# Layer 1's attention scores from float32 operands in groups of 32 rows, in a two-layer transformer kernel on one core

## What is computed

```python
# plain, and cosine with normalised q and k; a rotary turn came before
scores = einsum('bhtd,bhsd->bhts', q, k) * scale + causal
# hyperbolic
tq = sqrt(1 / curv + sum(q * q)); tk = sqrt(1 / curv + sum(k * k))
inner = einsum('bhtd,bhsd->bhts', q, k) - tq * tk.T
dis = sqrt(1 / curv) * arccosh(max(-curv * inner, 1 + 1e-7))
scores = 1 / (1e-6 + dis) + causal
# all
out = softmax(scores) @ v
```

## Time and profile before

| | |
|---|---|
| median of three executions | 2942.42 us |
| the profiled execution | 2944.73 us |
| its span, first to last instruction | 2942.8 us |
| mean granted clock of TensorE, of full speed | 0.814 |
| instructions | 30130 |
| DMA | 128.32 MB, 14.8% of 16 engines' span |

### The profile page before, as it was taken

One profiled execution on the slowest core, in us unless ns is written; L12 is line 12 of the kernel. 1 busy time (PEld: TensorE's weight loads), 2 busy tenths in 40 slices (PEclk: granted clock), 3 DMA queues, 4 the chain that ended last, 5 costly groups with the idle time before them and its releaser, 6 DMA issues. The chain is left out here.

```text
span 2942.8 us, 30130 instructions
## 1 busy us (share of the span) xinstructions
PE 2303.2 (78%) x10649; PEld 866.6 (29%) x10649; DVE 1553.3 (53%) x3429; ACT 1378.9 (47%) x1963; POOL 657.2 (22%) x639
## 2 busy tenths in 40 slices
PE   3799847777999884777798987667789998477789
PEld 1222321223433341122343234121334223212134
DVE  2553446675456354666455526467545634466642
ACT  1145315893134531788224452288622453248932
POOL 1012101332321210233241120033223111013324
PEclk8599866678999885777799987578689998667789
DMA  5100220001400022000330003110032002200012
GB/s 142 40 18 2 73 71 30 17 1 50 128 23 18 16 66 77 27 6 1 95 98 25 2 22 87 50 32 1 12 112 70 18 1 73 67 21 30 1 34 90
DMA packets 67750, 128.32 MB, mean 44 GB/s; under 512 B 11300, under 2 KB 24740, under 8 KB 62980
## 3 DMA queue, kind: packets, MB, share of 16 engines
q1 hardware_dynamic: 67600, 126.40, 14.8%
HBM read 109.99 MB, written 15.20 MB: 43 GB/s over the span
## 5 line engine op out<-in xcount | busy, mean ns | idle before, releaser
L1279 DVE TENSOR_REDUCE mx<-ps 128x1 f32<-128x512 f32 (+3 forms) x1248 | 644.0, 552 | 562.3 <-PE ps L629 468.6
L1008 ACT ACTIVATE pr<-ps 128x1024 f32<-128x1024 f32 (+3 forms) x672 | 515.9, 804 | 537.0 <-PE ps L699 534.4
L626 PE MATMUL ps<-kop,qop 72*128 72x512 bf16 (+6 forms) x1248 | 441.3, 372 | 158.2 <-DVE mx L1279 90.1
L699 PE MATMUL ps<-qop,kop 75*128 75x512 bf16 (+7 forms) x1344 | 409.8, 370 | 160.2 <-DMA kop<-parts_scratch 56.5
L745 PE MATMUL ps<-pr,vt 128*32 128x512 f32 (+3 forms) x2688 | 442.8, 590 | 5.2 <-POOL pr L1563 4.6
L1563 POOL TENSOR_SCALAR_AFFINE_SELECT pr<-pr 128x512 f32<-128x512 f32 x224 | 145.9, 651 | 987.5 <-ACT pr L1008 986.1
L1063 ACT ACTIVATE pr<-ps 128x512 f32<-128x512 f32 x224 | 133.8, 597 | 405.1 <-PE ps L851 316.4
L626 PEld LDWEIGHTS ps<-kop,qop 72*128 72x128 bf16 (+1 forms) x1248 | 124.7, 101 | 608.0 <-DVE mx L1279 342.8
L861 PE MATMUL ps<-pr,w_down 128*128 128x512 f32 x384 | 211.5, 638 | 69.6 <-POOL pr L1554 48.8
L699 PEld LDWEIGHTS ps<-qop,kop 75*128 75x128 bf16 (+1 forms) x1344 | 123.4, 105 | 380.3 <-ACT pr L1008 122.4
L848 PE MATMUL ps<-hT,w_gate 128*128 128x512 f32 x384 | 205.5, 618 | 0.0
(11 more groups left out here) (298 smaller groups left out, 3012.3 us busy)
## 6 DMA issues: line engine op xcount, KB each, us to landing
wb<-gates_scratch SPq DMA_DIRECT2D x192, 256.0 KB, 3.3
qop<-parts_scratch SPq DMA_DIRECT2D x96, 192.0 KB
kop<-parts_scratch SPq DMA_DIRECT2D x96, 192.0 KB
on<-hmax_scratch SPq DMA_DIRECT2D x8, 1024.0 KB, 5.5
parts_scratch<-on SPq DMA_DIRECT2D x24, 256.0 KB, 3.4
parts_scratch<-wb SPq DMA_DIRECT2D x24, 256.0 KB, 2.9
xin<-in_x SPq DMA_DIRECT2D x4, 512.0 KB, 4.5
on<-in_cos SPq DMA_DIRECT2D x4, 512.0 KB, 3.8
```

The lines of the kernel that those rows point to most:

```text
L626: mm = pe.matmul(o, qop[0:k, slot(l, u), j, qb * P:(qb + 1) * P], kop[0:k, slot(l, u), j, k0:k0 + wd], start=True, stop=not diag)
L699: mm = pe.matmul(o, kop[0:k, slot(l, u), 2 * pair + j, kb * P:(kb + 1) * P], qop[0:k, slot(l, u), 2 * pair + j, q0:q0 + wd], start=True, s ...
L1008: nc.scalar.activation(pr[:, g % 3, 2 * pair:2 * pair + 2, o0:o0 + wd], ps[:, bank:bank + 2, o0:o0 + wd], ACT.Exp).then_inc(a.exps, 1)
L1279: ins_ = nc.vector.tensor_reduce(mx[:, nth(l, u) % 2, j, qb, col % 2:col % 2 + 1], ps[:, bank, 0:wd], AX.X, ALU.max, negate=True)
```

## The change

In layer 1, q and k stay float32. `qop` and `kop` are seen as `q32` and `k32`, [128 rows, 4 units, 1024]; head j of a unit has rows 32j to 32j+7. Row 32j+8 (`MROW`) holds the row maximum in `q32` and ones in `k32`; for the hyperbolic unit row 32j+8 holds ones in both, and 32j+9 (`TROW`) holds tq or tk. 32 DMAs copy head by head from where q and k were computed. A score is one float32 product of 8, 9 or 10 rows, placed at row 32j of the array. The maxima of units 1 and 2 are turned in float32 and stored by one DMA. Layer 0 is as before, but its rows of ones are loaded again in each batch, since layer 1 overwrites them. The core of the diff:

```diff
+        q32, k32 = (op[:, 0:2].rearrange("p s j n -> p (s j n)").bitcast(F32).rearrange("p (u n) -> p u n", u=UNITS)
+                    for op in (qop, kop))
-        trow = [on[0:36, 3, 0:CH].bitcast(BF16), on[0:36, 2, 0:CH].bitcast(BF16)]
+        trow = [on[0:4, 1, :], on[0:4, 2, :]]
 setup, SP and POOL
+                sp.wait_ge(s_ones, 1)
+                sp.dma_start(ones_dram, k32[MROW::32]).then_inc(s_stored, 16)
+                sp.wait_ge(s_stored, 16)
+                sp.wait_ge(s_ones, 2)
-                nc.gpsimd.memset(kop[:], 1.0)
+                nc.gpsimd.memset(k32[:], 1.0).then_inc(s_ones, 1)
+                pool.wait_ge(s_stored, 16)
+                nc.gpsimd.memset(kop[:], 1.0).then_inc(s_ones, 1)
 PE, rows of tq and tk
-                            mm = pe.matmul(ps[0:36, (6 if side else 2) + t // 4, (t % 4) * P:(t % 4 + 1) * P],
-                                           tp9[:, t, side], identb[:], start=True, stop=True)
+                            col = 4 * (NT * side + t)
+                            mm = pe.matmul(ps[0:4, (6 if side else 2) + t // 4, (t % 4) * P:(t % 4 + 1) * P],
+                                           tT[:, col:col + 4], w["ident"][:], start=True, stop=True)
 PE, pieces
-                        mm = pe.matmul(o, qop[0:k, slot(l, u), j, qb * P:(qb + 1) * P],
-                                       kop[0:k, slot(l, u), j, k0:k0 + wd], start=True, stop=not diag)
+                        if l:
+                            rows = slice(32 * j, 32 * j + (TROW + 1 if is_hyp(l, u) else HD))
+                            mm = pe.matmul(o, q32[rows, u, qb * P:(qb + 1) * P], k32[rows, u, k0:k0 + wd],
+                                           start=True, stop=not diag, tile_position=(32 * j, 0))
 PE, scores (hyp_scores likewise, with TROW + 1)
+                            if l:
+                                rows = slice(32 * h, 32 * h + (MROW + 1 if has_max(l, u) else HD))
+                                mm = pe.matmul(o, k32[rows, u, kb * P:(kb + 1) * P], q32[rows, u, q0:q0 + wd],
+                                               start=True, stop=True, tile_position=(32 * h, 0))
 DVE, prepare: both splits go, and the split and copies of the rows of tq and tk
-                    dve.wait_ge(factors_used, i + 1)
-                    operand_parts(1, 3 * i, parts[:, i], dsts[i], tmp)
-                link(split(by_tile(tT), lambda k: tp[:, :, :, k, :], by_tile(tU)))
-                for i in range(3):
-                    nc.vector.tensor_copy(q9[:, :, i], tp[:, :, 0])
-                    ins_ = nc.vector.tensor_copy(k9[:, :, i], tp[:, :, 1, i].unsqueeze(2).broadcast_to([P, NT, 3, 4]))
 DVE, maxima of standard units: no split
+                    if l and not is_hyp(l, u):
+                        ins_.then_inc(a.nmp, 1)
+                        return
 SP
+            def move_heads(side, u):
+                src, dst = (on[:, 0, :], kT[:])[side], (q32, k32)[side]
+                for j in range(4):
+                    h = HD * (4 * u + j)
+                    sp.dma_start(dst[32 * j:32 * j + HD, u, :], src[h:h + HD, :]).then_inc(at[1].ops[u], 16)
 SP, send_maxima
+                if l:
+                    sp.dma_start(q32[MROW::32, u, :].rearrange("j (q n) -> j q n", n=P),
+                                 hrow[:]).then_inc(at[1].maxrow[u], 16)
+                    return
 SP, layer 0's start; before layer 0's gates; after them
+                sp.dma_start(kop[MAXROW:MAXROW + 3, 0:2].rearrange("p s j n -> p s (j n)"),
+                             ins["onerow"][0:1].rearrange("a j n -> a (j n)").unsqueeze(1).broadcast_to(
+                                 [3, 2, 4 * N])).then_inc(at[0].one_rows, 16)
-            sp.dma_start(qop[MAXROW:MAXROW + 3, slot(1, HYP_UNIT), :, :], ins["onerow"]).then_inc(
-                at[1].ops[HYP_UNIT], 16)
+            sp.dma_start(k32[MROW::32], ones_dram).then_inc(at[1].one_rows, 16)
+            sp.dma_start(q32[MROW::32, HYP_UNIT, :], ones_dram[:, 0]).then_inc(at[1].one_rows, 16)
             for side in range(2):
-                store_parts(1, side, 3 * side, parts[:, side])
-            for u in (0, HYP_UNIT, 1):
-                load_unit(1, u)
+                sp.wait_ge(factors_used, side + 1)
+                for u in (0, HYP_UNIT, 1, 2):
+                    move_heads(side, u)
+            for dst, row, ready in ((q32, trow[0], t_row), (k32, trow[1], t_krow)):
+                sp.wait_ge(ready, 1)
+                sp.dma_start(dst[TROW::32, HYP_UNIT, :], row).then_inc(at[1].ops[HYP_UNIT], 16)
             for c in range(NC):
                 spread_hyp_maxima(c)
             send_maxima(1, b + 1 < B, 1, BOTH)
-            sp.wait_ge(at[1].pv, NS)
-            load_unit(1, 2)
             send_maxima(1, b + 1 < B, 2, BOTH)
```

More of the change, by code:

```diff
@@ L18 @@
 MAXROW = PAIRS
-TROW = PAIRS + 3
-K_MAX, K_HYP = PAIRS + 3, PAIRS + 3 + 9
+K_MAX = PAIRS + 3
 LN_EPS = 1e-5
@@ L46 @@
 NP_ = len(PIECES)
-OPS = 16 * 6
-OPS_HYP = OPS + 16 * (1 + 2)
+OPS = (16 * 6, 16 * 8)
+OPS_HYP = OPS[1] + 16 * 2
+MROW, TROW = HD, HD + 1
 def diagonals(g):
@@ L481, in __init__ @@
                     self.proj, self.proj_used = sem(n + "proj"), sem(n + "proj_used")
-                self.parts = sem(n + "parts")
-                self.stored = [sem(n + f"stored{i}") for i in range(2)]
+                else:
+                    self.parts = sem(n + "parts")
+                    self.stored = [sem(n + f"stored{i}") for i in range(2)]
+                self.one_rows = sem(n + "one_rows")
                 self.v = sem(n + "v")
@@ L714, in hyp_scores @@
                     for j in range(2):
[L715 to L718, removed]
+                        h = 2 * (k % 2) + j
+                        rows = slice(32 * h, 32 * h + TROW + 1)
+                        mm = pe.matmul(ps[:, bank + j, o0:o0 + wd], k32[rows, HYP_UNIT, kb * P:(kb + 1) * P],
+                                       q32[rows, HYP_UNIT, q0:q0 + wd], start=True, stop=True,
+                                       tile_position=(32 * h, 0))
                     mm.then_inc(h_prod, 1)
@@ L1126, in split, with operand_parts @@
                 return nc.vector.tensor_tensor(dst(2), r, dst(1), ALU.subtract)
-            def operand_parts(l, first, p, src, r):
-                done = at[l].parts
+            def operand_parts(first, p, src, r):
+                done = at[0].parts
                 nc.vector.tensor_copy(p[:, 0, :], src).then_inc(done, 1)
@@ L1232, in maxima @@
                                                        ALU.min)
+                    if l and not is_hyp(l, u):
+                        ins_.then_inc(a.nmp, 1)
+                        return
                     link(ins_)
-                    if is_hyp(l, u):
+                    if l:
                         c = chunks[0]
@@ L1619, in sync_program, with load_rows @@
         def sync_program(sp, b):
-            def load_rows(l, u, side, i):
+            def load_rows(u, side, i):
                 op = (qop, kop)[side]
-                heads = scratch[l, side, :, :, 4 * u:4 * u + 4, :].rearrange("i d h n -> i d (h n)")
+                heads = scratch[side, :, :, 4 * u:4 * u + 4, :].rearrange("i d h n -> i d (h n)")
                 if side:
@@ L1627, in load_rows, with load_unit, store_parts @@
                     src = heads.rearrange("i d n -> (i d) n")
[L1628 to L1633, removed]
+                sp.dma_start(op[24 * i:24 * i + 24, slot(u), :, :].rearrange("p h n -> p (h n)"),
+                             src).then_inc(at[0].ops[u], 16)
+            def load_unit(u):
                 for side in range(2):
                     if u == 0:
-                        sp.wait_ge(a.stored[side], 48)
+                        sp.wait_ge(at[0].stored[side], 48)
                     for i in range(3):
[L1638 to L1641, removed]
-                        sp.dma_start(op[TROW:TROW + 9, slot(l, u), :, :], rows).then_inc(a.ops[u], 16)
-            def store_parts(l, side, first, p):
+                        load_rows(u, side, i)
+            def move_heads(side, u):
[3 more added lines that the diff above has]
+                    sp.dma_start(dst[32 * j:32 * j + HD, u, :], src[h:h + HD, :]).then_inc(at[1].ops[u], 16)
+            def store_parts(side, first, p):
                 for i in range(3):
-                    sp.wait_ge(at[l].parts, first + i + 1)
-                    sp.dma_start(scratch[l, side, i].rearrange("d h n -> h d n"), p[:, i]).then_inc(
-                        at[l].stored[side], 16)
+                    sp.wait_ge(at[0].parts, first + i + 1)
+                    sp.dma_start(scratch[side, i].rearrange("d h n -> h d n"), p[:, i]).then_inc(
+                        at[0].stored[side], 16)
             def gate_rows(l, guest):
```

78 lines of the change are left out of this document (42 added, 36 removed).

## The result

The changed kernel takes 3576.64 us (median of four runs, 3575.58 to 3581.00), against 2942.96 for the kernel before: 1.2159 times as long, 95% interval 1.2135 to 1.2182. The forecast was 2928, its range ended at 3035. Two executions of the kernel before, beside the first run of experiment 8, were in a slow state (3703.63 and 8405.29 us) and are left out of its median.

What follows compares the result with a forecast made beforehand. PE was busiest overall, but the stage had an empty start, a lower-clock PE stretch and ScalarE-bound stretches. -19.3 and +14.5 gave -4.8 a batch, -19 in four; with +4.5 setup, 2928 us, range 2862 to 3035.

Steps and rivals of the forecast that it cites:

- Term 1: Start of layer 1's attention stage: bf16 splits go and first pieces start earlier, about -19.3 us per batch.
- Term 3: Setup, once: POOL fills k32, waits for its store, then fills kop; DVE last before; +4.5 us.
- Term 2: PE's work in layer 1's attention stage: float32 columns cost four times bf16's, partly regained by overlap; +14.5 us a batch.
- The lower clock that slows it now should go once PE has no gaps.: Positions 2 to 5 of the stage: 39.8 us becomes 42, +2, with the lower clock expected to go.
- that cover would just do: Positions 22 to 27, 36.1 us: hidden by ScalarE's 34.46 even if PE stayed at the lower clock; change 0.
- Three of the signs named beforehand: Forecast wrong if stretches grow over 25 us a batch or nothing, or POOL's fill doesn't end after DVE; clock near 1 expected.
- every rival: Whole kernel: forecast case 2900 to 2960 us (0.43); others 2876 (0.19), 3002 (0.20), 3110 (0.12), 2967 (0.06).
- Rival D: Layer 1's attention: row groups don't overlap, pairs run in series, 18.5 plus 27 us a batch, 3110 us; chance 0.12.
- Work in columns: PE's stage work counted at the upper clock: 1.67 ns a float32 column, 0.42 a bf16 one.
- Pairs overlap: Adjacent score pairs in different row groups overlap as column groups do: 0.98 us start to start, not 1.72.
- Pieces hidden, a quarter to a third: Pieces in another row group hide beside score pairs: 2, 5, 4.5, 3 and 7 us by stretch.
- Tile changes, 0.22 us a mask at the upper clock: Two more tile changes of about 0.11 us at each mask product, 80 a stage: 18 us.

Runs made afterwards that it cites:

- experiment 8: Kernel before with q's loads moved ahead of k's stores: alone 2923.56 us (ratio 0.9925); with layer 1's products also widened to 128 rows 2883.44 us (0.9787).
- Experiment 7: Kernel before, layer 1's scores and pieces reading 128 rows instead of 72 to 84, added q rows zero: 2888.55 us against 2941.21, ratio 0.9809.
- experiment 3: Changed kernel, layer 1's float32 scores and pieces each reading all 128 rows, no row groups, nothing overlapping, scores not the reference's: 3146.93 us.
- experiment 4: Changed kernel with bf16 on the same rows: everything, from constants, 2940.44 us; only pieces 3146.30 us; only scores 3325.43 us.
- experiment 1: Changed kernel, each row group's products reading all 32 rows instead of 8 to 10: added q rows zero 3374.11 us; holding 0.001, 3440.39 us.
- experiment 5: Changed kernel with layer 1's pieces lacking their mask products: 3414.17 us.

## Why the prediction was wrong

**Term 1, the start, was right, its size in part by luck.** The first piece comes 20.1 us earlier in the first batch, counted from the first clamp, and 19.8 to 21.6 in the others, against 19.3 forecast; position 0's exponential comes 14.4 to 15.4 us earlier in each batch (forecast for its scores: 13.4). Two parts were off and nearly cancelled. The row transposes (L615) took 5.97 us, not 7.5. A move took 0.67 us, not 0.35, so the row copies stood behind k's moves until 417.6. With the 6.3 us by which the setup put the batch off, that is 411.3 on the clock of the old trace, against the forecast's 410:

```profile
396.16 10.73 SPq L1664 DMA_DIRECT2D qop<-on  x16
406.93 10.63 SPq L1664 DMA_DIRECT2D kop<-kT  x16
417.61 0.53 SPq L1765 DMA_DIRECT2D qop<-on  x1
```

**Term 3, the setup: +4.5 forecast, +6.3 to the first clamp.** POOL's fill ended at 46.5, to the tenth. What I had wrong is who is last behind it. The timeline of the setup, all engines:

```profile
36.18 10.34 POOL L415 MEMSET kop<- 128x12288 bf16 x1 [31.83 <-DMA ones_scratch<-kop]
38.41 0.18 DVE L459 COPY mod<-ps 128x24 f32<-128x24 f32 x1 [3.09 <-PE ps L437]
38.63 8.14 DVE L461 TENSOR_SCALAR mod<-mod 128x4 f32<-128x4 f32 x2
...
48.62 0.16 DVE L468 SCALAR_TENSOR_TENSOR mod<-nr 128x4 f32<-128x4 f32 x1
```

Two DVE operations on four elements took 8.14 us and ended with POOL's fill; DVE's remaining ten come after it, so DVE still is the last engine. The same operation took 0.17 us in the kernel before, with no fill beside it. The fill doesn't lie beside DVE's work, it stops it.

**Term 2 is where it failed, and by one step:** "The lower clock that slows it now should go once PE has no gaps." The gaps went and the clock fell: 96% busy at 0.51 over the first stage, and 669 us more in the four stages where 14.5 a batch were forecast. I had the rows of both in hand, 72 and 84 rows, and a clock of 0.59 at 80% busy in the earlier trace rows, and read the second as a matter of gaps. Experiment 7 shows it was at least in part the rows read; experiment 3 shows the same order of work at 0.97. The forecast gave the lower clock no rival of its own; the only sentence on it dealt with positions 22 to 27 ("that cover would just do"): 45.5 us there, not 36.1. Three of the signs named beforehand came: the stretches grew by over 25 us a batch, the clock wasn't near 1 in positions 2 to 21, and POOL's fill didn't end after DVE. The kernel's time lies beyond every rival, D's 3110 too.

The other steps of term 2, by the runs:
- *Work in columns.* Serial and at a clock of 0.97 the stage took 313.8 us (experiment 3). Rival D, no overlap at the upper clock, made it 252.5 - 5.9 + 14.5 + 18.5 + 27 = 306.6, the 5.9 being the part of term 1 that lies behind the first exponential (19.3 less 13.4). The 18 us of tile changes in that sum are not in this kernel, so the rest was undercounted by some 25 us, 8% of the stage.
- *Pairs overlap.* Right, and D is wrong: they start within 0.01 us of each other, and four heads at once where their banks are free.
- *Pieces hidden, a quarter to a third.* The mechanism is in the timeline, a piece beside two scores; its size stays open, as experiment 4 says. In positions 16 to 21 the 32-row kernel at 0.89 took 65.3 us; I had forecast 56.
- *Tile changes, 0.22 us a mask at the upper clock.* 0.51 in all at the lower clock, the mask's stream among it; no run prices it at the upper.

Had the clock stayed up, the forecast would still have been too low, but by some 36 to 100 us in the whole kernel and not by over six hundred. That is an estimate from positions 16 to 21 in experiment 1, 9 us a batch over, and from the 25 of experiment 3.

## What to carry to other kernels

Read the granted clock of each stage together with the rows that its products use: where it is low although PE is busy, try the same instructions on more rows, with zeros in the added ones, before touching anything else. Here it cost PE nothing and gave 1.9%. Packing products of few rows side by side divides their time, but it can leave every product of the stage at half the clock, so price such a change at the lower clock, and count four passes of float32 at that clock too.

## What the runs showed that was not expected

- Rows against clock, in the first batch's stage: 8 to 10 rows 0.51, also one at a time; 32 rows in row groups 0.64; 72 to 84 rows of bf16 0.71; these widened to 128 by zeros 0.85; 128 rows of float32 0.97. PE was busy 96, 93, 74, 68 and 93% of it. The order follows the rows and not the busy share. Rows are not all of it: 8 to 10 rows of bf16 had 0.60 at 77% busy, and 32 rows had 0.57 in one batch of four.
- The low clock reaches products that use all 128 rows when they stand among narrow ones: L769, 128 rows and 32 columns, took 1061 ns a half in this stage and L745 took 830 before.
- At the upper clock a float32 product of 512 columns on 128 rows takes 0.86 us (432.41 to 433.27 in experiment 5's timeline); four heads in four row groups took 1.14 together, in a short stretch of the changed kernel in which the clock was at 1.00 until its last 0.1 us.
- A fill by POOL held a DVE operation of four elements for 7.9 us. The Trainium skill (SBUF — State Buffer, SBUF: two separate sides) describes an exclusive lock on a shared port pair between the two engines, held for a whole instruction, for some kinds of DVE operations. The trace agrees: the operation took 7.92 us, until 0.03 us after the fill, and 0.17 in the kernel before. The copy from PSUM at 38.41 ran in 0.18 us during the same fill.
